# A decoder layer on one core: two norms applied by VectorE, a weight copied in halves, the first key projection moved, the start reordered

## What is computed

```
h  = layernorm(x) * g + b                       # norm "a"
p  = relu(h @ K.T) ** 2 ; x = x + x + p @ V     # 4 heads of 64, 1024 keys and values, from weights
x  = layernorm(x)                               # norm "b"
Q  = x Wq + bq ; K = ctx Wk + bk ; V = ctx Wv   # 16 heads of 16
A  = softmax(Q K / 4 + alpha_pos * max(D, 0) + alpha_neg * min(D, 0))    # D = clipped f[k] - f[q]
x  = layernorm(x + (A V) Wo + bo)               # norm "c"
u  = lowrank(x, expert chosen by argmax(x gate))
x  = layernorm(x + relu(x Wi + u B) Wo2 + wo_b) # norm "d"
```

## Time and profile before

| | |
|---|---|
| median of three runs | 880.25 us |
| the profiled execution, whole run | 880.8 us |
| its span (first to last instruction) | 879.0 us |
| PE busy | 856.4 us, 97% of the span |
| DVE, ACT, POOL busy | 758.8, 713.7, 588.3 us |
| mean granted clock of TensorE | 0.994 of full speed |

### The profile page before, as it was taken

One profiled execution on the slowest core, in us unless ns is written; L12 is line 12 of the kernel. 1 busy time (PEld: TensorE's weight loads), 2 busy tenths in 40 slices (PEclk: granted clock), 3 DMA queues, 4 the chain that ended last, 5 costly groups with the idle time before them and its releaser, 6 DMA issues.

```text
span 879.0 us, 20994 instructions
## 1 busy us (share of the span) xinstructions
PE 856.4 (97%) x7194; PEld 686.9 (78%) x7194; DVE 758.8 (86%) x2161; ACT 713.7 (81%) x1948; POOL 588.3 (67%) x762
## 2 busy tenths in 40 slices
PE   8999899999999999999999999999999999999996
PEld 6666577778778787877878787787778778788786
DVE  5868989989898898989889898988989888899953
ACT  5569898898888978888897988889798888878841
POOL 6667877777767776766777676677768676654411
PEclk9999999999999999999999999999999999999999
DMA  6333222122231222222122222312212221222200
GB/s 169 99 61 67 52 53 44 38 42 43 58 71 43 44 52 41 55 58 58 43 44 55 38 55 59 58 44 43 56 37 55 58 58 31 38 56 40 47 13 25
DMA packets 40187, 46.15 MB, mean 53 GB/s; under 512 B 10417, under 2 KB 27313, under 8 KB 40082
## 3 DMA queue, kind: packets, MB, share of 16 engines
q1 hardware_dynamic: 40082, 44.82, 25.4%
HBM read 15.42 MB, written 4.19 MB: 22 GB/s over the span
## 4 chain that ended last, share of the span: by engine, by line
PE 88%; ACT 5%; DVE 3%; SPq 2%; issue 1%; DMA 1%; POOLq 0%; DVEq 0%; POOL 0%; ACTq 0%
PE bank L401 12%; PE bank L297 12%; PE bank L482 10%; PE bank L250 10%; PE bank L414 7%; PE bank L392 7%; PE bank L285 6%; PE bank L286 6%; PE bank L370 3%; ACT P L699 2%; PE bank L351 2%; PE bank L331 2%; PE bank L492 2%; PE bank L376 2%; PE bank L317 1%; ACT STG L621 1%
## 5 line engine op out<-in xcount | busy, mean ns | idle before, releaser
L1167 POOL TENSOR_SCALAR U<-DP,alph 128x512 f32<-128x512 f32 x256 | 193.5, 757 | 123.0 <-DVE NM L919 67.9
L699 ACT ACTIVATE P<-T,NM 128x256 f32<-128x256 f32 x512 | 256.4, 511 | 1.4 <-DVE NM L919 1.3
L1149 POOL TENSOR_TENSOR R<-R 128x512 f32<-128x512 f32 x208 | 221.5, 1065 | 40.0 <-ACT R L645 39.7
L912 DVE SCALAR_TENSOR_TENSOR bank<-DN,alph,bank 128x512 f32<-128x512 f32 x256 | 190.3, 743 | 29.3 <-PE bank L392 27.6
L919 DVE CUSTOM_DVE_ANT_0 T<-bank,U 128x256 f32<-128x256 f32 x512 | 197.0, 422 | 9.5 <-DVE bank L912 0.7
L621 ACT ACTIVATE STG<-bank 128x512 f32<-128x512 f32 x256 | 152.5, 596 | 42.8 <-PE bank L401 41.7
L645 ACT ACTIVATE R<-bank 128x512 f32<-128x512 f32 x248 | 147.2, 597 | 24.9 <-PE bank L286 22.9
L401 PE MATMUL bank<-ident,P 128*128 128x128 f32 x1024 | 156.1, 275 | 5.1 <-ACT STG L621 4.8
L401 PEld LDWEIGHTS bank<-ident,P 128*128 128x128 f32 x1024 | 118.4, 140 | 29.9 <-ACT P L699 13.4
L297 PE MATMUL bank<-R,VS 128*32 128x512 f32 x992 | 118.4, 593 | 0.0
L392 PE MATMUL bank<-QS 128*128 128x256 f32 x512 | 110.4, 297 | 2.3 <-DVE NM L919 1.9
(11 more groups left out here) (183 smaller groups left out, 1854.8 us busy)
## 6 DMA issues: line engine op xcount, KB each, us to landing
QS<-QK SPq DMA_DIRECT2D x384, 64.0 KB, 2.4
XG<-in_x SPq DMA_DIRECT2D x16, 256.0 KB, 3.1
CT<-in_ctxT SPq DMA_DIRECT2D x16, 256.0 KB, 2.9
out<-XO SPq DMA_DIRECT2D x15, 256.0 KB, 2.5
FK<-in_frac SPq DMA_DIRECT2D x16, 128.0 KB, 3.4
STG<-in_wiT SPq DMA_DIRECT2D x2, 512.0 KB, 5.1
STG<-in_woT SPq DMA_DIRECT2D x2, 512.0 KB, 4.1
STG<-in_kT SPq DMA_DIRECT2D x2, 256.0 KB, 4.5
```

Source lines behind the costliest of these rows:

```text
L699: eng.activation(P[n % NP][:, cs], T[n % NT][:, cs], ACT.Exp, bias=NM[:, n % 8, q:q + 1], scale=-1.0, accum_out=SU[n // 16 % 2][:, q, seat ...
L912: eng.scalar_tensor_tensor(out=L[:, :], in0=dn[:, :], scalar=alph[:, 16 + h:17 + h], in1=L[:, :], op0=ALU.mult, op1=ALU.add).then_inc(s_t1, 1)
L1149: eng.tensor_tensor(r, r, r, ALU.mult).then_inc(s_sqp, 1)
L1167: eng.tensor_scalar(U[n % NU][:, :], dp[:, :], alph[:, h:h + 1], 0.0, ALU.mult, ALU.add).then_inc(s_u, 1)
```

## The change

Two norms change hands. In batch 0, norm b is now applied by DVE (`centred("b", 0, X1, XG[0], s_x1)`, subtract the mean and multiply, two instructions) and not by ACT; in batch 15, norm c is applied whole by DVE, ahead of `y3` of batch 14. POOL's two shift products fall away for these two (set `DIRECT`). The key weight `KH` is copied by ACT in two halves. `kp(0)` and what belongs to it moves from between batch 1's scores to between batch 0's scores 6 and 7. The numbers of nearly all lines change by a little; as an order of instructions that is mostly a new order of the start, some changes in the last batch, and a few swaps of neighbours per batch in between.

```diff
+        DIRECT = (("b", 0), ("c", NB - 1))
 # ACT
             def x1(b):
+                if b == 0:
+                    return
-                act.wait_ge(s_nm["b"], 2 * b + 2)
+                act.wait_ge(s_nm["b"], 2 * b)
             def x2(b):
+                if b == NB - 1:
+                    return
-                for t in range(1 if b == NB - 1 else 2):
+                for t in range(2):
-            weight("kT", KH[:, :], stage(1024, 0))
+            for half in (slice(0, 512), slice(512, 1024)):
+                weight("kT", KH[:, half], stage(1024, 0)[:, half])
...
-                if g == -862:
+                if g == -930:
                     act.wait_ge(s_wqs, 1)
                     weight("q", W["q"][0][:, :, :], view(512, 0, 128, 2))
-                for b, _ in due(g, -244, early=-10, late=48):
+                for b, _ in due(g, -244, early=-647, late=61):
                     projected("kp", b, 2, 2, s_kp, s_kh)
 # DVE
-            def weight(name, lo, src, hi):
-                dve.wait_ge(s_whi[name], 1)
+            def weight(name, lo, src, hi, piece=0):
+                dve.wait_ge(s_whi[name], piece + 1)
-            def last_x2():
...
+                if g == -348:
+                    centred("b", 0, X1, XG[0], s_x1)
+                for b, _ in due(g, 1065, start=15, late=-115):
+                    dve.wait_ge(s_x2T, b)
+                    dve.wait_ge(s_x2b, b)
+                    centred("c", b, X2, X1b[b % 2], s_x2)
-                if g == 10708:
-                    last_x2()
-                if g == -793:
+                if g == -1181:
                     dve.wait_ge(d_small, 160)
                     eng.tensor_scalar(bqk[:, 0:2], bqk[:, 0:2], gd[:, 0:1], 0.25, ALU.mult, ALU.mult)
                     eng.tensor_scalar(alph[:, :], alph[:, :], gd[:, 1:2], None, ALU.mult).then_inc(s_small, 1)
-                for b, _ in due(g, -290, early=-39, late=81):
+                for b, _ in due(g, -286, early=-900, late=78):
                     cl(b)
-                for b, _ in due(g, -235, early=-48, late=52):
+                for b, _ in due(g, -235, early=-793, late=70):
                     projected("kp", b, 2, 2, s_kh, s_kl)
 # POOL
-                if k in "bc":
+                if k in "bc" and (k, b) not in DIRECT:
 # PE
-                for b, _ in due(g, -246, early=-38, late=47):
+                for b, _ in due(g, -241, early=-788, late=51):
                     kp(b)
```

More of the change, by code:

```diff
@@ new lines, in _ @@
+                if g == -923:
+                    pe.wait_ge(s_id, 1)
+                    filler(6, pV)
+                if g == -643:
+                    pe.wait_ge(s_id, 1)
+                    filler(3, pV)
+                if g == -500:
+                    pe.wait_ge(s_id, 1)
+                    filler(4, pV)
+                if g == -303:
+                    pe.wait_ge(s_id, 1)
+                    filler(16, pV)
+                if g == -188:
+                    pe.wait_ge(s_id, 1)
+                    filler(2, pV)
@@ L561, in _ @@
                     pe.wait_ge(s_ot, NB)
                     filler(1, pA)
[L563 to L569, removed]
+                for b, u in due(g, -7, 16, 39, early=4, late=7):
                     logits(16 * b + u)
-                for b, u in due(g, 1322, 4, 25, early=-21, late=382):
+                for b, u in due(g, 1316, 4, 27, early=-19, late=348):
@@ L610, in _ @@
                     xnT(0)
-                if g == -640:
+                if g == -688:
                     xnT(1)
-                for b, _ in due(g, -1224, start=2, late=-8):
+                for b, _ in due(g, -1221, start=2, late=1):
                     xnT(b)
@@ L754, in _ @@
                     x1(b)
-                for b, u in due(g, 84, 16, 39, early=-15, late=4):
+                for b, u in due(g, 84, 16, 39, early=-8, late=1):
                     exps(16 * b + u)
-                if g == -1409:
+                if g == -1554:
                     skh(0)
-                if g == -596:
+                if g == -578:
                     skh(1)
-                for b, _ in due(g, -1214, start=2, late=-14):
+                for b, _ in due(g, -1221, start=2, late=13):
@@ L1016, in _ @@
                     y1(b)
-                for b, u in due(g, 1311, 4, 31, early=-15, late=538):
+                for b, u in due(g, 1311, 4, 31, early=-15, late=526):
                     il(b, u)
-                if g == -2479:
+                if g == -2272:
                     dve.wait_ge(d_x[0], 16)
                     stats("a", 0, XG[0])
-                if g == -2133:
+                if g == -2223:
                     centred("a", 0, XN, XG[0], s_x0)
-                if g == -963:
+                if g == -1136:
@@ L1037, in _ @@
+                if g == -1330:
                     dve.wait_ge(d_x[1], 16)
                     stats("a", 1, XG[1])
-                for b, _ in due(g, -1504, start=2, late=23):
+                for b, _ in due(g, -1498, start=2, late=51):
                     dve.wait_ge(d_x[b % 2], 16 * (b // 2 + 1))
                     stats("a", b, XG[b % 2])
-                for b, _ in due(g, 673, early=1):
+                for b, _ in due(g, 654, early=33, late=20):
                     rc(b)
-                for b, _ in due(g, 811, early=-28, late=-12):
+                for b, _ in due(g, 811, early=-14, late=25):
@@ L1045, in _ @@
                     ao(b)
-                for b, _ in due(g, 870, early=-28, late=-25):
+                for b, _ in due(g, 862, early=-37, late=28):
                     aol(b)
-                if g == -1756:
+                if g == -1938:
                     skl(0)
-                if g == -772:
+                if g == -827:
                     skl(1)
-                for b, _ in due(g, -1233, start=2, late=-8):
+                for b, _ in due(g, -1228, start=2, late=6):
                     skl(b)
-                for b, _ in due(g, 1617, early=-9, late=962):
+                for b, _ in due(g, 1622, early=9, late=756):
@@ L1055, in _ @@
                     y3(b)
-                for b, _ in due(g, 2026, early=-134, late=959):
+                for b, _ in due(g, 2038, early=-17, late=462):
                     dve.wait_ge(d_o, 16 * b)
@@ L1114, in _ @@
                     ull(b)
-                for b, u in due(g, -1134, 16, 37, early=-182, late=61):
+                for b, u in due(g, -1134, 16, 37, early=-109, late=27):
                     if on_dve(b, u):
@@ L1220, in _ @@
                     plus(X1b[b % 2], X1, boB, s_x1b)
-                for b, _ in due(g, 1427, early=-73, late=646):
+                for b, _ in due(g, 1405, early=178, late=258):
                     pool.wait_ge(s_x2, 2 * b + 2)
@@ L1226, in _ @@
                     plus(X2b, X2, woB, s_x2b)
-                for b, u in due(g, -1078, 16, 37, early=62, late=-28):
+                for b, u in due(g, -1076, 16, 37, early=101, late=-30):
                     if not on_dve(b, u):
```

271 lines of the change are left out of this document (126 added, 145 removed).

## The result

Four runs of the changed kernel took 874.72 to 875.4 us, median 874.94; four of the kernel before, on the same chip, 878.56 to 880.57, median 880.16. The ratio is 0.9943, with a 95% interval of 0.993 to 0.9956: 5.2 us faster, where 4.0 was forecast. The profiled execution took 875.4 us (before 880.8), its span is 873.6 us (879.0), so these two differ by 5.4 us.

A forecast was written before the change was run, and what follows sets the result against it. PE, busy 599.86 of 600 us from 140 to 740 us, bounds the kernel, so only start and end can give: -1.3 - 2.7 = -4.0 us, from 880.25 to 876.2 us; own range 874.7 to 877.6, with rivals 873.2 to 879.3.

The forecast's parts named there:

- The end: After op: x2T without a wait, 3.0 us earlier; `ffn_in(15)` 2.5 us earlier; a 0.24 us wait gone; -2.7 us.
- Step 1: Start: two fewer fillers and `first_gain` done first bring the first scores some 1.5 us earlier, 9.9 against 11.36 us.
- Step 2: Start: DVE scales Wq in 0.43 us, not 1.70; ACT gets it at 18.25 us, 1.2 us earlier.
- Step 3: Start: s0.8 and av0.0 wait for work queued behind Wq's copy and low part, 1.55 and 0.6 us; about +2.1 us.
- Steps 4 to 6: Start: otT(0) 0.3 us later at 39.1, x1T 1.35 earlier at 46.7, restack 1.3 earlier at 52.4 us.
- Step 7: From the first logits to 140 us: nearly the same order of the same work, so the start's lead is carried on.
- C: Rival: PE's pauses from 17.8 to 20.95 us bring half speed; start +1.6, end -2.7, 879.1 us; chance 0.12.
- B: Rival: the start gives nothing and the end all, 877.5 us; chance 0.17.
- D: Rival: in the steady state a blocked third `restack` or waiting DVE stalls PE, 0.5 us per batch; 883.3 us; chance 0.08.
- PE idle in the steady state: Sign that the forecast is wrong: any idle of PE in the steady state.
- the same lead at 140 us: Sign for the forecast: the lead at restack, near 52.4 us, still there unchanged at 140 us.

The follow-up runs named there:

- start only: Changed kernel up to batch 7, the last eight batches with the order of the kernel before; 878.34 us, ratio 0.9989.
- the two with fillers: Kernel before with five fillers in the gap at 106 us, or 15 instead of 8 ahead of the first scores; 880.0 and 880.46 us.
- the one with `values` behind: Kernel before with values(0,3) moved behind the turn of batch 1's unit 0 and one scores tile; 879.9 us, ratio 0.9999.
- end only: Kernel before up to batch 7, the last eight batches with the changed order; 875.5 us, ratio 0.9953.
- the changed kernel once more: The changed kernel, unaltered, run again beside the kernel before on the same chip; 876.19 us, ratio 0.9956.

## Why the prediction was right, and where not

The forecast of 4.0 us lies between the two measurements, 5.2 and 3.6 us. By its steps:

- **The end**, forecast -2.7: measured -3.05 between the profiles. op's end to x2T 7.26 to 4.08 us (forecast 3.0 less, was 3.18), to `ffn_in(15)` 9.73 to 7.10 (2.5, was 2.63), the rest 0.42 and not 0.24. The mechanism was right. What the step didn't contain is the clock: I took the 1.65 us pause at x2T as harmless because the earlier trace rows showed no fall behind it. It falls behind that pause in the profiles of four kernels that keep it (start only, and the two with fillers and the one with `values` behind), where x2T to the end of the span takes 22.6 to 22.9 us and not 21.4. So taking the pause away gives 1.2 to 1.5 us more in such executions; that fits the 4.3 us of the end alone.
- **Step 1**, first scores at 9.9: came at 10.50. `first_gain` does come first, but the two fillers saved nothing: 30 records took 5.76 us until xnT at 7.27, 34 before 5.62.
- **Step 2**, scaling 0.43, Wq on ACT at 18.25: 0.49 and 18.21.
- **Step 3**, waits of 1.55 and 0.6 us at s0.8 and av0.0: the times were right (19.38 and 20.99, forecast 19.4 and 20.95), the place was not. The stop is ahead of kp's low part, 1.49 us for `CL`, which DVE makes in 1.52 us beside POOL; I had counted kp as twelve matmuls without asking when `CL` is there. Two slips of the sum did no harm: the 5.8 us for eight tiles "as before" held some 3.5 us at half speed (seven tiles took 3.75 us here, at full speed), and 18.85 + 0.7 + 0.75 + 0.7 is 21.00 and not 20.95. Wq decides when s0.8 and av0.0 can run, not PE's arrival.
- **Steps 4 to 6**: otT(0) 39.12 (39.1), x1T 46.65 (46.7), restack 52.54 (52.4), first logits 59.53 (59.3). So close a hit is the hit of one execution: with Wq late, the same list gave 61.93 and 60.66 us.
- **Step 7, the lead is carried on**, held where it can be read: 0.45 us at the first logits and 0.5 to 0.8 us from there to 773 us, between end only and the changed kernel. What was mis-sized is the lead that it carries, -1.3 in the sum. In the forecast's own pair it was 1.1 us, of which 0.66 lay in before's execution (first logits at 60.64 us, in end only at 59.98 with the same order); and it became 2.9 because that execution had a clock fall at 107 us, which the sum had no term for. Over five profiles each, the mean lead at the first logits is 0.01 us; the medians of start only say 1.5 us, with an interval that reaches 0. That the sum came out near is partly luck: a start of -1.3 that is worth 0.5 to 0.8 us without falls, and an end of -2.7 that is worth -3 plus the falls it avoids.
- **The rivals.** C, with its pauses and its clock, is real in single executions (the changed kernel once more). B (the start gives nothing) describes the start well, though not the time. D did not come: PE is busy 600.00 of 600 us; the store stands ahead of the third restack (411.52 us in its batch) and costs nothing. "PE idle in the steady state" was the right thing to watch, "the same lead at 140 us" was the criterion that broke, by the clock.

## What to carry to other kernels

Ask of every pause of PE not only how long it is but what runs behind it: one at full speed in the trace can be at half speed in the next execution, and work moved into a pause (here a projection) is then worth more than its own time. Compare a landmark per stage in both traces; a lead that jumps where nothing was changed is not the change's. And when a transfer lands at a time that varies, take out from behind it, on each in-order engine, all that doesn't need it.

## What the runs showed of the hardware

- The granted clock fell after some pauses and not after others of the same length and place: 1.42 us at 107 us yes in the profile of before, 1.43 and 1.42 at the same place of the same order no (end only, and the kernel with 15 fillers); 1.65 us at x2T no in the profile of before and yes in start only; 1.49 us at kp's low part no in the changed kernel and yes in start only. After such a pause it stayed at 1.2 GHz for some 3 to 4 us (12 to 15.6 and 107.5 to 111 us in the profile of before). The fall at 107 us cost 1.5 us. The one at 12 us cost nothing that these profiles show: the kernel with `values` behind a turn has it too, and its batch 1's `otT` comes at 70.49 us, against 70.44 and 70.55 in the two with fillers, which don't have it. Of the 80 runs of before, 24 had a mean granted clock of 0.999 or more and averaged 878.9 us, 23 had 0.996 or less and averaged 881.0. What decides a single case stays open. The Trainium skill (TensorE: Matmul & The Clock Gate, "Part 1: The HAM clock gate") has the clock drop after idling; the traces agree in so far as each fall that cost time stood behind a pause, but of the 35 pauses of 1.29 to 1.95 us in the fourteen profiles only 11 had a fall at their end or behind them.
- DVE's low part of a 128x512 tile took 0.69 us with POOL idle (11.10 us, the second of `KL`) or 1.52 while POOL squared (`CL`, 15.66 us); the scaling of Wq 0.49 or, while POOL squared and cleared a tile, 1.70; a one-row weight 1.21 with POOL idle or 2.06 while it squared. The Trainium skill (SBUF — State Buffer, "SBUF: two separate sides") says the two take turns on one pair of ports; these pairs agree.
